# Block transposes on VectorE and sixteen copies in place of TensorE transposes, for three of four batches

## The chip, the cores and the metric

The kernel runs on one core of a Trainium2 chip. The metric is the device time of one execution in microseconds; of the kernel before there are three timed runs and one profiled execution.

## The reference

The inputs are x (4 batches of 512 tokens, 512 wide, float32) and a context of the same shape.

```
xn   = (x - mean) / sqrt(var + eps)                      # layer norm
q, k_new, v_new = xn @ wq.T, xn @ wk.T, xn @ wv.T
k, v = concat(ctx, k_new), concat(ctx, v_new)            # 1024 keys
x    = x + softmax(q @ k.T / sqrt(512)) @ v @ wo.T
xf   = layer_norm(x)
w, idx = top_k(softmax(xf @ gate.T), 6)                  # 64 experts, capacity 128
x    = x + routed experts(xf, w, idx) + shared expert(xf)
```

Every product is done as three passes over numbers split into a high and a low part (high by high, high by low, low by high), each part in a one-pass format. So every operand of TensorE exists twice, as `name_hi` and `name_lo`: ScalarE makes the high part by a copy with rounding, VectorE makes the low part by subtracting the high part from the value.

## The kernel before

**Stages.** Attention and router run batch by batch, then the 64 experts. The function `body` of each engine handles batch b and, while it does, prepares batch b+1: its rows x are loaded, normalised, transposed to `xnT` and projected to q, k and v. Batch 0's own preparation stands ahead of the loop. The last call has `more` false and prepares no batch.

**TensorE's order in a body** (L968 on): transposes of the softmax rows (`pT`), the scores of row tiles 2 and 3, the projections v 1 to 3 of batch b (the last readers of this batch's `xnT`), four groups `av` of 24 matmuls each (attention times values), four groups `wo` of 12 matmuls (the output projection), q 0 and 1 of batch b+1, transposes `x2T` of the second norm, q 2 and 3, the router's logits, k 0 to 3, v 0, the scores of row tile 0, eight short matmuls `pos` that count how many earlier tokens chose each expert, and the scores of row tile 1. In the kernel before, the transposes of the normalised rows stand in this order too: tiles 0 and 1 after `av` 1, tiles 2 and 3 after `av` 3, four 128x128 transposes a tile, by `transposes` at L901 (matmuls against an identity, into a PSUM bank).

**Groups and banks.** Every such product is a group, and the groups take four PSUM banks in turn, by the list `groups_of` (L50). A group's bank is free when the group four places ahead of it has been taken: ScalarE writes the high part (`high`, L447), VectorE subtracts and adds one to `group_taken` (`low`, L578). TensorE waits for that in `claim`; `taken` waits until an operand has been split. The order in which ScalarE and VectorE take groups is written out in their bodies as calls `h(...)` and `l(...)`.

**Weights and context** come through two stage buffers of 1 MB as items, in the order `ctx`, `wo`, `ctxT'`, `wq'`, `wk'`, `wv'`; SyncE loads an item when VectorE has made the low part of the item two places ahead (`load_item`, L287). `high_item` and `low_item` split them, 2048 columns at a time.

**The normalised rows.** `xn` is one tile of 128 partitions by 4 by 512. It is also the router's scratch: `hot` (24 one-hot rows of 64) and `chosen` (the mask) are views of it. At L309 SyncE loads the next rows once all groups of the last body are taken, the two of `pos` among them. VectorE takes statistics (`layernorm_stats`, L585) after v 3, GpSimd raises the variance to the power -1/2 (`first_norm`, L395), and VectorE normalises in place (`layernorm_apply`, L596) after `av` 0.

**The router's mask.** L797 sums the six one-hot rows of each token by four reductions; L800 and L802 make the mask and its running sums, after which TensorE's `pos` group may start (`chosen_ready`). L817 then picks positions with 24 small instructions a batch whose main output goes to `hot` and is not read (only the accumulated column is).

**GpSimd** sends the routed tokens of a batch to the table by 24 indirect DMAs (L421), during the next body. Each waits for a step of TensorE's pace (`paced`: two steps for each scores tile, one for each v group, two for each av group). The norm's power stands in that list ahead of DMA 12.

Of the kernel before, what the change touches and what calls it, by code (L numbers as in the profile page):

```python
# [29 lines left out]
P = 128  # L30
# [11 lines left out]
OVER = float(1 << 20)  # L42

# [6 lines left out]
def groups_of(more):  # L50

    nxt = more * 1
    return (
        [("pT", n) for n in range(6)] + [("v", 1), ("pT", 6), ("pT", 7), ("v", 2), ("v", 3)]
        + [("av", 0), ("av", 1)] + [("xnT", 0), ("xnT", 1)] * nxt + [("av", 2), ("av", 3)]
        + [("xnT", 2), ("xnT", 3)] * nxt + [("wo", i) for i in range(NT)]
        + [("q", 0), ("q", 1)] * nxt + [("x2T", i) for i in range(NT)] + [("q", 2), ("q", 3)] * nxt
        + ([("logitsT", 0), ("k", 0), ("logits", 0), ("k", 1), ("k", 2), ("k", 3), ("v", 0), ("pos", 0), ("pos", 1)]
           if more else [("logits", 0), ("logits", 1), ("pos", 0), ("tab", 0), ("tabw", 0)])
    )  # L60
# [41 lines left out]
def attention_and_router(nc, ctx, sem, t, table, x2_rows, second_sum, x2T_kept, kept):  # L102
# [21 lines left out]
    x2T = tuple(h[:, 0:C, :] for h in pT)  # L124
    pbuf = sb("pbuf", [P, 2, KV])
    x2 = pbuf[:, :, :].rearrange("p a (b d) -> p (a b) d", d=D)
    xn = sb("xn", [P, NT, D])
    logitsT = xn[0:E, 0, :]
# [70 lines left out]
    xn_ready = sem("xn_ready")  # L199
    scores_full = sem("scores_full")  # L200
# [39 lines left out]
    ctx_v = t["ctx"].rearrange("(b i p) d -> b p i d", b=B, p=P)  # L240
    weight_source = {"wq'": t["wqT"], "wk'": t["wkT"], "wv'": t["wvT"], "wo": t["woT"],
# [43 lines left out]

    def sync(sp, before_last_rows):
# [16 lines left out]
        def body(b, more):  # L303
            load_item(b, more, "ctx", b)
            load_item(b, more, "wo")
            if more:

                sp.wait_ge(group_taken, b * PER + len(FIRST) + BANKS)
                sp.dma_start(xn[:, :, :], x_v[b + 1]).then_inc(x_loaded, 16)  # L309
# [3 lines left out]
            if more:  # L313
                for name in ("ctxT'", "wq'", "wk'"):
                    load_item(b, more, name, b + 1)
# [43 lines left out]
    def gpsimd(pool):  # L359
# [40 lines left out]
        def body(b, more):  # L400
# [35 lines left out]
    def scalar(act, two):  # L436
# [21 lines left out]
        def body(b, more):  # L458
# [9 lines left out]
            exp(b, 3)  # L468
            h(("pT", 4), ("pT", 5), ("v", 1), ("pT", 6), ("pT", 7), ("v", 2), ("v", 3))
# [92 lines left out]
    def vector(dve, two):  # L562
# [22 lines left out]
        def layernorm_stats(by_tile=False):  # L585
            for i in range(NT):
                if by_tile:
                    dve.wait_ge(x_tile_loaded[i], 16)
                last = dve.bn_stats(stats[:, i, :], xn[:, i, :])
            link(last)  # L590
            for i in range(NT):
# [101 lines left out]
        def body(b, more):  # L693
# [25 lines left out]
            l(("av", 0))  # L719
            if more:  # L720
                dve.wait_ge(rstd_ready, b * (NT + 1) + 2)
                layernorm_apply()
            l(("av", 1))
# [7 lines left out]
            if more:  # L731
                l(("xnT", 2), ("xnT", 3))
# [63 lines left out]
            for i in range(NT):  # L796
# [14 lines left out]
            for n in range(2):  # L811
# [3 lines left out]
                for i in (2 * n, 2 * n + 1):  # L815
                    for k in range(K):
                        last = dve.scalar_tensor_tensor(  # L817
                            out=hot[:, i * K + k, :], in0=iota_e[:, :], scalar=argf[:, i, k:k + 1],
# [20 lines left out]
        layernorm_stats(by_tile=True)  # L839
# [21 lines left out]
    def tensor(pe, two):  # L861
# [106 lines left out]
        def body(b, more):  # L968
# [5 lines left out]
            def next_xnT(*tiles):  # L974
                for i in tiles:
                    pe.wait_ge(xn_ready, (b + 1) * NT + i + 1)
                    transposes(b, more, ("xnT", i), xn[:, i, :])

# [10 lines left out]
            for m in range(C):  # L989
# [23 lines left out]
            if more:  # L1013
                taken(b, more, ("xnT", NT - 1))
# [787 lines left out]
```

## Time and profile before

| | us |
|---|---|
| median of 3 timed runs | 806.75 (806.72 to 806.81) |
| the profiled execution | 804.55 |
| its span, first to last instruction | 802.8 |
| TensorE busy | 767.4 (96%) |
| VectorE busy | 592.1 (74%) |
| ScalarE busy | 449.4 (56%) |
| GpSimd busy | 319.6 (40%) |

The engines' busy times overlap, so they do not add up to the span. PE is TensorE's matmul side, DVE is VectorE, ACT is ScalarE, POOL is GpSimd, SP is SyncE, which only issues DMAs here; a q behind a name is the engine's instruction queue. Matmuls are pipelined: one of 512 columns is shown as 0.39 us long, while the next starts 0.23 us after it, so time on TensorE is read from the starts. A body lasts 99 us: the first stands at about 50 to 150 us, the second at 150 to 249 and the third at 249 to 348.

### The profile page before, as it was taken

The numbers are of one execution on the slowest core, as the hardware profiler recorded it, in microseconds if no ns is written. First come the engines' busy times: TensorE is split into PE (matmuls) and PEld (weight loads), VectorE is DVE, ScalarE is ACT, GpSimd is POOL, SyncE is SP. The second block draws the span as 40 slices with busy tenths as digits, with TensorE's granted clock in tenths as the row PEclk, the third lists the DMA queues.
The fourth block names the chain that finished last, engine by engine and source line by source line (L and its number), as shares of the span: only waits on it lengthen the run. The fifth ranks groups of instructions, "written<-read, shape, count | busy, mean of one in ns | idle before, by whom it ended". The sixth has DMA issues, their size and how long they took to land.

```text
span 802.8 us, 10922 instructions
## 1 busy us (share of the span) xinstructions
PE 767.4 (96%) x3886; PEld 648.9 (81%) x3886; DVE 592.1 (74%) x1174; ACT 449.4 (56%) x795; POOL 319.6 (40%) x256
## 2 busy tenths in 40 slices
PE   6999999999999999999999999999999999999982
PEld 5888887888878887888888888898988888888762
DVE  6437485875867757676478799999999989999622
ACT  3424323343233333334243799999899888889610
POOL 1000010337103461045423656556565676565440
PEclk9999999999999999999999999999999999999997
DMA  5961236222453225503284999999999999999988
GB/s 167 318 246 54 105 150 217 88 74 103 177 191 106 69 90 200 219 2 109 86 322 158 285 355 343 355 353 344 350 347 351 347 345 349 344 352 349 251 175 195
DMA packets 60292, 181.39 MB, mean 226 GB/s; under 512 B 7680, under 2 KB 8064, under 8 KB 56576
## 3 DMA queue, kind: packets, MB, share of 16 engines
q1 hardware_dynamic: 41184, 139.74, 46.5%
q0 software_dynamic: 19056, 40.98, 22.0%
q8 instruction: 31, 0.51, 0.2%
q14 instruction: 21, 0.17, 0.1%
HBM read 144.38 MB, written 43.92 MB: 235 GB/s over the span
## 4 chain that ended last, share of the span: by engine, by line
PE 59%; DMA 16%; DVE 10%; issue 5%; ACT 4%; POOL 4%; SPq 1%; POOLq 0%; DVEq 0%
PE bank L1097 8%; PE bank L1099 8%; PE bank L1098 8%; DMA raw<-expert_in 7%; DMA stage<-wvT_in 3%; PE scores L1097 3%; PE scores L1099 3%; PE scores L1098 3%; PE ps_gu L1097 3%; PE ps_gu L1099 3%; PE ps_gu L1098 3%; PE bank L904 3%; DMA second_sum<-product,idx_all 3%; DMA second_sum<-eo,idx_all 2%; PE ps_dn L1097 2%
## 5 line engine op out<-in xcount | busy, mean ns | idle before, releaser
L421 POOL DMA_INDIRECT table<-rows,slot x72 | 80.4, 1117 | 157.8 <-DVEq L831 114.1
L1482 DVE TENSOR_TENSOR gu_lo<-raw,gu_hi 128x768 fp32r<-128x768 f32 x126 | 120.3, 956 | 12.9 <-ACT gu_hi L1398 12.1
L1398 ACT ACTIVATE gu_hi<-raw 128x768 fp32r<-128x768 f32 x128 | 107.3, 841 | 10.9 <-DMA raw<-expert_in 10.6
L1097 PE MATMUL ps_gu<-gu_hi,xgT_hi 128*128 128x384 f32 x256 | 91.5, 357 | 0.0
L1099 PE MATMUL ps_gu<-gu_hi,xgT_lo 128*128 128x384 f32 x256 | 86.4, 337 | 0.0
L1098 PE MATMUL ps_gu<-gu_lo,xgT_hi 128*128 128x384 f32 x256 | 86.1, 336 | 0.0
L449 ACT ACTIVATE qT<-bank 128x512 fp32r<-128x512 f32 x32 | 19.2, 600 | 114.7 <-PE bank L1099 109.1
L1342 POOL DMA_INDIRECT xg<-x_rows,idx_all x39 | 47.4, 1216 | 42.3 <-DVEq L667 17.4
L454 ACT ACTIVATE pbuf<-scores,negmax 128x1024 f32<-128x1024 f32 x16 | 17.9, 1118 | 70.2 <-DVE negmax L604 70.2
L582 DVE TENSOR_TENSOR qT<-bank,qT 128x512 fp32r<-128x512 f32 x32 | 22.1, 690 | 47.1 <-ACT qT L449 47.1
L1350 POOL DMA_INDIRECT out_rows<-product,idx_all x25 | 41.3, 1651 | 31.6 <-DMA out_rows<-product,idx_all 14.5
L1098 PEld LDWEIGHTS ps_gu<-gu_lo,xgT_hi 128*128 128x128 f32 x256 | 48.3, 189 | 0.0
L1097 PEld LDWEIGHTS ps_gu<-gu_hi,xgT_hi 128*128 128x128 f32 x256 | 48.2, 188 | 0.0
L1099 PEld LDWEIGHTS ps_gu<-gu_hi,xgT_lo 128*128 128x128 f32 x256 | 48.1, 188 | 0.0
L1482 DVE TENSOR_TENSOR dn_lo<-raw,dn_hi 128x512 fp32r<-128x512 f32 x64 | 44.1, 688 | 2.4 <-ACT dn_hi L1403 1.9
L1482 DVE TENSOR_TENSOR dn_hi<-rest,dn_hi 64x512 fp32r<-64x512 f32 x64 | 44.0, 688 | 0.9
L1097 PE MATMUL bank<-xnT_hi,w_hi 128*128 128x512 f32 x112 | 44.2, 395 | 0.0
L1482 DVE TENSOR_TENSOR xgT_lo<-ps_xgT,xgT_hi 128x512 fp32r<-128x512 f32 x64 | 43.8, 684 | 0.2 <-ACT xgT_hi L1417 0.2
L1099 PE MATMUL bank<-xnT_hi,w_lo 128*128 128x512 f32 x112 | 43.7, 390 | 0.0
L1098 PE MATMUL bank<-xnT_lo,w_hi 128*128 128x512 f32 x112 | 43.6, 389 | 0.0
L398 POOL TENSOR_TENSOR rstd<-veps,half 128x4 f32<-128x4 f32 x4 | 9.9, 2469 | 84.6 <-DVE veps L594 84.6
L582 DVE TENSOR_TENSOR pT_lo<-bank,pT_hi 128x512 fp32r<-128x512 f32 x48 | 30.5, 684 | 16.7 <-ACT pT_hi L449 16.6
(284 smaller groups left out, 2267.5 us busy)
## 6 DMA issues: line engine op xcount, KB each, us to landing
raw<-expert_in SPq DMA_DIRECT2D x64, 1024.0 KB, 13.6
rest<-rest_in SPq DMA_DIRECT2D x32, 256.0 KB, 10.0
x_rows<-pbuf SPq DMA_DIRECT2D x17, 256.0 KB, 2.3
stage<-wkT_in SPq DMA_DIRECT2D x4, 1024.0 KB, 4.9
stage<-ctxT_in SPq DMA_DIRECT2D x4, 1024.0 KB, 4.8
stage<-wvT_in SPq DMA_DIRECT2D x4, 1024.0 KB, 9.0
stage<-ctx_in SPq DMA_DIRECT2D x4, 1024.0 KB, 9.4
stage<-woT_in SPq DMA_DIRECT2D x4, 1024.0 KB, 4.9
```

The lines of the kernel that those rows point to most:

```text
L421: pool.indirect_dma_start(out=table, out_offset=bass.IndirectOffsetOnAxis(ap=slot[:, i, k:k + 1], axis=0), in_=rows[:, i, k, :], in_offset ...
L449: act.activation(split_dest(group)[0], split_source(key, group), ACT.Copy).then_inc(high_done, 1)
L454: act.activation(pbuf[:, i % 2, :], scores[:, i % 2, :], ACT.Exp, bias=negmax[:, i:i + 1], scale=SCALE, accum_out=rowsum[:, i:i + 1]).then ...
L582: dve.tensor_tensor(lo, split_source(key, group), hi.bitcast(F32), ALU.subtract).then_inc(group_taken, 1)
L904: last = pe.transpose(bank_of(key, group)[:, cols(j)], source[:, cols(j)], ident[:, :])
L1097: pe.matmul(out, still[0], moving[0], start=first, stop=False)
L1098: pe.matmul(out, still[0], moving[1], start=False, stop=False)
L1099: return pe.matmul(out, still[1], moving[0], start=False, stop=last)
L1342: pool.indirect_dma_start(out=xg[e % XG], out_offset=None, in_=x2_rows, in_offset=index(("expert", e))).then_inc(gathered[e % XG], 16)
L1350: pool.indirect_dma_start(out=(t["out"], second_sum)[r % 2], out_offset=index(what), in_=eo[r % EO], in_offset=None, compute_op=ALU.add).t ...
L1398: act.activation(gu[n % GU_SLOTS][0][part], gate_up_of(n, part), ACT.Copy).then_inc(weights_high, 1)
L1482: return dve.tensor_tensor(lo, x, hi.bitcast(F32), ALU.subtract)
```

## The change

1. The eight TensorE transposes after `av` 1 and the eight after `av` 3 are gone, with their groups, in the three bodies with `more`.
2. In their place VectorE transposes every 32x32 block of the normalised rows into `blocks`, a view of `pbuf` (the softmax rows, read by then), four instructions of 128x512 after v 3. Sixteen DMAs of 64 KB, each 32 partitions by 4 by 128 numbers, carry the blocks to their partitions, into `xnT_lo`: eight issued by SyncE, eight by ScalarE after it has taken `av` 0. ScalarE then rounds `xnT_lo` into `xnT_hi` and VectorE subtracts in place, four instructions of 128x512 each, after `av` 1 and item `ctxT'`. The rows are loaded in another order of tokens (`x_quads`) so that this comes out right.
3. The load of the next rows, as four DMAs, is issued when the mask of the last batch is made, ahead of item `wo` on SyncE's queue. For this the unread output of L817 goes to a free part of `pT_hi`, and ScalarE waits for the end of that stage (`rows_ready`) before `pT` 4.
4. The statistics are taken earlier: two tiles after the maximum of row tile 2, two after `pT` 3, the variances after the maximum of row tile 3. The rows are normalised after v 2. GpSimd's power stands ahead of DMA 9 instead of DMA 12.
5. The mask is summed by three additions over all tiles (768, 256 and 256 columns) instead of four reductions.

```diff
@@ groups_of
-        + [("av", 0), ("av", 1)] + [("xnT", 0), ("xnT", 1)] * nxt + [("av", 2), ("av", 3)]
-        + [("xnT", 2), ("xnT", 3)] * nxt + [("wo", i) for i in range(NT)]
+        + [("av", m) for m in range(C)] + [("wo", i) for i in range(NT)]
...
+    unused = [pT[0][:, C + m // 4, (m % 4 + 4) * E:(m % 4 + 5) * E] for m in range(2 * K)]
+    blocks = pbuf[:, :, :].rearrange("p a k -> p (a k)").rearrange("p (d t j) -> p d t j", t=NT, j=SQ)
...
+    def tokens_of(a):
+        return tuple(h[:, :, a * P:(a + 1) * P] for h in xnT)
+
+    def move_xnT(queue, b, first, past):
+        queue.wait_ge(group_full, place(b, True, ("v", C - 1)) + 1)
+        queue.wait_ge(xn_blocked, (b + 1) * NT)
+        for a in range(first, past):
+            for q in range(QUADS):
+                here = blocks[a * SQ:(a + 1) * SQ, :, :, :].rearrange("p (c q) t j -> p q c (t j)", q=QUADS)
+                queue.dma_start(plain(tokens_of(a)[1][q * SQ:(q + 1) * SQ, :, :]),
+                                here[:, q, :, :]).then_inc(xnT_moved[a], 16)
@@ SyncE
             load_item(b, more, "ctx", b)
+            if more:
+                if b:
+                    sp.wait_ge(chosen_ready, b)
+                    sp.wait_ge(router_exp, b * 2 * NT)
+                else:
+                    sp.wait_ge(group_taken, place(0, "first", ("xnT", NT - 1)) + 1 + BANKS)
+                for a in range(QUADS):
+                    sp.dma_start(xn[a * SQ:(a + 1) * SQ, :, :], x_quads[b + 1, a]).then_inc(x_loaded, 16)
             load_item(b, more, "wo")
-            if more:
-                sp.wait_ge(group_taken, b * PER + len(FIRST) + BANKS)
-                sp.dma_start(xn[:, :, :], x_v[b + 1]).then_inc(x_loaded, 16)
...
-                for name in ("ctxT'", "wq'", "wk'"):
+                load_item(b, more, "ctxT'", b + 1)
+                move_xnT(sp, b, 0, 2)
+                for name in ("wq'", "wk'"):
@@ GpSimd
-                if i == 2 and b + 2 < B:
-                    first_norm((b + 1) * (NT + 1) + 1)
                 for k in range(K):
+                    if i * K + k == 9 and b + 2 < B:
+                        first_norm((b + 1) * (NT + 1) + 1)
@@ ScalarE
+            act.wait_ge(rows_ready, 2 * b)
             h(("pT", 4), ("pT", 5), ("v", 1), ("pT", 6), ("pT", 7), ("v", 2), ("v", 3))
...
-            h(("av", 0), ("av", 1))
-            if more:
-                h(("xnT", 0), ("xnT", 1))
+            h(("av", 0))
+            if more:
+                move_xnT(act, b, 2, QUADS)
+            h(("av", 1))
+            if more:
                 high_item(b, more, "ctxT'")
+                for a in range(QUADS):
+                    act.wait_ge(xnT_moved[a], (b + 1) * 16 * QUADS)
+                    hi, lo = tokens_of(a)
+                    act.activation(hi, plain(lo), ACT.Copy).then_inc(xnT_high, 1)
             h(("av", 2), ("av", 3))
             if more:
-                h(("xnT", 2), ("xnT", 3))
@@ VectorE
             maximum(b, 2)
+            if more:
+                dve.wait_ge(x_loaded, (b + 1) * 16 * QUADS)
+                tile_stats(0, 2)
             l(("pT", 2), ("pT", 3))
+            if more:
+                tile_stats(2, NT)
             maximum(b, 3)
+            if more:
+                variances()
...
-            l(("v", 2), ("v", 3))
-            if more:
-                dve.wait_ge(x_loaded, (b + 1) * 16)
-                layernorm_stats()
+            l(("v", 2))
+            if more:
+                dve.wait_ge(rstd_ready, b * (NT + 1) + 2)
+                layernorm_apply()
+            l(("v", 3))
+            if more:
+                for i in range(NT):
+                    dve.wait_ge(xn_ready, (b + 1) * NT + i + 1)
+                    dve.transpose(blocks[:, :, i, :], xn[:, i, :].rearrange("p (d j) -> p d j", j=SQ)
+                                  ).then_inc(xn_blocked, 1)
...
-                l(("xnT", 0), ("xnT", 1))
                 low_item(b, more, "ctxT'")
+                for a in range(QUADS):
+                    dve.wait_ge(xnT_high, b * QUADS + a + 1)
+                    hi, lo = tokens_of(a)
+                    dve.tensor_tensor(lo, plain(lo), plain(hi), ALU.subtract).then_inc(xnT_low, 1)
...
-            for i in range(NT):
-                last = dve.tensor_reduce(chosen[:, i, :], hot[:, i * K:(i + 1) * K, :]
-                                         .rearrange("p k e -> p e k"), AX.X, ALU.add)
-            link(last)
+            hot_of = hot.rearrange("p (i k) e -> p i k e", k=K)
+            link(dve.tensor_tensor(hot_of[:, :, 0:3, :], hot_of[:, :, 0:3, :], hot_of[:, :, 3:6, :], ALU.add))
+            link(dve.tensor_tensor(hot_of[:, :, 0, :], hot_of[:, :, 0, :], hot_of[:, :, 1, :], ALU.add))
+            link(dve.tensor_tensor(chosen[:, :, :], hot_of[:, :, 0, :], hot_of[:, :, 2, :], ALU.add))
@@ TensorE
-                if more and m == 1:
-                    next_xnT(0, 1)
-            if more:
-                next_xnT(2, 3)
...
-                taken(b, more, ("xnT", NT - 1))
+                pe.wait_ge(xnT_low, (b + 1) * QUADS)
                 item(b, more, "wq'")
```

## Rows read from the trace of the kernel before

**Rows 1.** The page: engine totals, then granted TensorE clock and DMA share in 40 slices.
```profile
PE 767.4 (96%) x3886; PEld 648.9 (81%) x3886; DVE 592.1 (74%) x1174; ACT 449.4 (56%) x795; POOL 319.6 (40%) x256
PEclk9999999999999999999999999999999999999997
DMA  5961236222453225503284999999999999999988
```
**Rows 2.** TensorE's waits over the span: us in total, times, longest.
```profile
PE bank L904 <- DVE qT L582: 0.6, 3, 0.2
PE bank L1051 <- DVEq L803: 0.6, 3, 0.2
```
**Rows 3.** TensorE in order of time, body 0, av to wo: start, duration in us.
```profile
73.77 0.39 PE L1097 MATMUL bank<-pT_hi,cx 128*128 128x512 f32 x1
...
76.49 0.39 PE L1097 MATMUL bank<-pT_hi,v_hi 128*128 128x512 f32 x1
...
84.42 0.39 PE L1099 MATMUL bank<-pT_hi,v_lo 128*128 128x512 f32 x1
84.65 1.03 PE L904 MATMUL bank<-ident,xn 128*128 128x128 f32 x8
85.44 0.48 PE L1097 MATMUL bank<-pT_hi,cx 128*128 128x512 f32 x1
85.76 0.40 PE L1098 MATMUL bank<-pT_lo,cx 128*128 128x512 f32 x1
...
96.43 1.03 PE L904 MATMUL bank<-ident,xn 128*128 128x128 f32 x8
97.22 0.48 PE L1097 MATMUL bank<-w_hi,qT 128*128 128x512 f32 x1
97.53 0.40 PE L1098 MATMUL bank<-w_lo,qT 128*128 128x512 f32 x1
```
**Rows 4.** TensorE in order of time at the mask, end of body 0.
```profile
143.23 0.39 PE L1098 MATMUL scores<-kT_lo,qT 128*128 128x512 f32 x1
143.45 0.39 PE L1099 MATMUL scores<-kT_hi,qT 128*128 128x512 f32 x1
144.02 0.20 PE L1051 MATMUL bank<-chosen_b,before 128*128 128x64 bf16 x1 [0.18 <-DVEq L803]
```
**Rows 5.** VectorE in order of time at the mask.
```profile
139.59 3.07 DVE L797 TENSOR_REDUCE xn<-xn 128x64 f32<-128x384 f32 x4
142.70 0.29 DVE L800 CAST chosen_b<-xn 128x256 bf16<-128x256 f32 x1
```
**Rows 6.** Additions of 768 and 256 columns elsewhere: ns min/median/max, first and last start.
```profile
L1482 DVE TENSOR_TENSOR gu_lo<-raw,gu_hi x126: 948/955/1019, 439.1 to 752.3; 128x768 fp32r<-128x768 f32 x126
L635 DVE TENSOR_TENSOR product<-xn x3: 418/419/424, 417.8 to 418.4; 128x256 f32<-128x256 f32 x3
```
**Rows 7.** VectorE in order of time, body 0; in brackets idle before and releaser.
```profile
60.52 1.29 DVE L582 TENSOR_TENSOR pT_lo<-bank,pT_hi 128x512 fp32r<-128x512 f32 x2 [1.76 <-ACT pT_hi L449]
63.67 1.23 DVE L603 TENSOR_REDUCE mx<-scores 128x1 f32<-128x1024 f32 x1 [1.87 <-PE scores L1099]
66.85 1.29 DVE L582 TENSOR_TENSOR pT_lo<-bank,pT_hi 128x512 fp32r<-128x512 f32 x2 [1.76 <-ACT pT_hi L449]
74.60 0.69 DVE L582 TENSOR_TENSOR v_lo<-bank,v_hi 128x512 fp32r<-128x512 f32 x1 [1.87 <-ACT v_hi L449]
75.21 2.46 DVE L589 BATCH_NORM_STATS2 stats<-xn 128x6 f32<-128x512 f32 x4
78.19 2.29 DVE L575 TENSOR_TENSOR w_lo<-stage,w_hi 128x2048 fp32r<-128x2048 f32 x1
81.39 1.92 DVE L598 TENSOR_SCALAR xn<-xn,mv,rstd 128x512 f32<-128x512 f32 x4 [0.31 <-POOL rstd L398]
97.26 0.69 DVE L582 TENSOR_TENSOR qT<-bank,qT 128x512 fp32r<-128x512 f32 x1 [4.76 <-ACT qT L449]
```
**Rows 8.** ScalarE in order of time, body 0, taking av 0 to av 2.
```profile
79.41 0.60 ACT L449 ACTIVATE qT<-bank 128x512 fp32r<-128x512 f32 x1 [3.04 <-PE bank L1099]
84.85 0.60 ACT L449 ACTIVATE qT<-bank 128x512 fp32r<-128x512 f32 x1 [4.84 <-PE bank L1099]
91.18 0.60 ACT L449 ACTIVATE qT<-bank 128x512 fp32r<-128x512 f32 x1 [2.95 <-PE bank L1099]
```
**Rows 9.** DMA issues over the span: times, KB each, median us to landing.
```profile
tab<-table SPq DMA_DIRECT2D x1, 64.0 KB, 2.7
stage<-wqT_in SPq DMA_DIRECT2D x3, 1024.0 KB, 4.8
```
**Rows 10.** The line that loads x's first four tiles: issue ns, then landing.
```profile
L336 SPq DMA_DIRECT2D xn<-x_in x4: 388/424/432, 0.9 to 2.3; - x4
DMA to landing us min/median/max: 2.7/3.5/4.4
```
**Rows 11.** GpSimd in order of time, body 1: DMA 8, then the norm's power.
```profile
162.73 0.97 POOL L421 DMA_INDIRECT table<-rows,slot  x1 [1.75 <-PE scores L1099]
...
177.44 2.95 POOL L398 TENSOR_TENSOR rstd<-veps,half 128x4 f32<-128x4 f32 x1 [5.46 <-DVE veps L594]
```

More of the change, by code:

```diff
@@ L42 @@
 OVER = float(1 << 20)
+SQ = 32
+QUADS = P // SQ
 BANKS = 4
@@ L199, in attention_and_router @@
     xn_ready = sem("xn_ready")
+    xn_blocked = sem("xn_blocked")
+    xnT_moved = [sem(f"xnT_moved{a}") for a in range(QUADS)]
+    xnT_high = sem("xnT_high")
+    xnT_low = sem("xnT_low")
     scores_full = sem("scores_full")
@@ L240, in attention_and_router @@
     ctx_v = t["ctx"].rearrange("(b i p) d -> b p i d", b=B, p=P)
+    x_quads = t["x"].rearrange("(b a i j) d -> b a j i d", b=B, a=QUADS, j=SQ)
     weight_source = {"wq'": t["wqT"], "wk'": t["wkT"], "wv'": t["wvT"], "wo": t["woT"],
@@ L583, in low, with tile_stats, first_stats, variances @@
                               ALU.subtract).then_inc(group_taken, 1)
-        def layernorm_stats(by_tile=False):
-            for i in range(NT):
-                if by_tile:
-                    dve.wait_ge(x_tile_loaded[i], 16)
+        def tile_stats(first, past):
+            for i in range(first, past):
                 last = dve.bn_stats(stats[:, i, :], xn[:, i, :])
             link(last)
+        def first_stats():
+            for i in range(NT):
+                dve.wait_ge(x_tile_loaded[i], 16)
+                last = dve.bn_stats(stats[:, i, :], xn[:, i, :])
+            link(last)
+        def variances():
             for i in range(NT):
@@ L707, in body @@
             maximum(b, 2)
+            if more:
+                dve.wait_ge(x_loaded, (b + 1) * 16 * QUADS)
+                tile_stats(0, 2)
             l(("pT", 2), ("pT", 3))
+            if more:
+                tile_stats(2, NT)
             maximum(b, 3)
+            if more:
+                variances()
             l(("pT", 4), ("pT", 5), ("v", 1), ("pT", 6), ("pT", 7))
             low_item(b, more, "ctx")
-            l(("v", 2), ("v", 3))
+            l(("v", 2))
             if more:
-                dve.wait_ge(x_loaded, (b + 1) * 16)
-                layernorm_stats()
+                dve.wait_ge(rstd_ready, b * (NT + 1) + 2)
+                layernorm_apply()
+            l(("v", 3))
+            if more:
+                for i in range(NT):
+                    dve.wait_ge(xn_ready, (b + 1) * NT + i + 1)
+                    dve.transpose(blocks[:, :, i, :], xn[:, i, :].rearrange("p (d j) -> p d j", j=SQ)
+                                  ).then_inc(xn_blocked, 1)
             low_item(b, more, "wo")
@@ L718, in body @@
                 low_item(b, more, "sg")
-            l(("av", 0))
+            l(("av", 0), ("av", 1))
             if more:
-                dve.wait_ge(rstd_ready, b * (NT + 1) + 2)
-                layernorm_apply()
-            l(("av", 1))
-            if more:
-                l(("xnT", 0), ("xnT", 1))
                 low_item(b, more, "ctxT'")
+                for a in range(QUADS):
+                    dve.wait_ge(xnT_high, b * QUADS + a + 1)
+                    hi, lo = tokens_of(a)
+                    dve.tensor_tensor(lo, plain(lo), plain(hi), ALU.subtract).then_inc(xnT_low, 1)
             else:
@@ L731, in body @@
             if more:
-                l(("xnT", 2), ("xnT", 3))
                 low_item(b, more, "wq'")
@@ L795, in body @@
                 l(("k", 2), ("k", 3))
-            for i in range(NT):
-                last = dve.tensor_reduce(chosen[:, i, :], hot[:, i * K:(i + 1) * K, :]
-                                         .rearrange("p k e -> p e k"), AX.X, ALU.add)
-            link(last)
+            hot_of = hot.rearrange("p (i k) e -> p i k e", k=K)
+            link(dve.tensor_tensor(hot_of[:, :, 0:3, :], hot_of[:, :, 0:3, :], hot_of[:, :, 3:6, :], ALU.add))
+            link(dve.tensor_tensor(hot_of[:, :, 0, :], hot_of[:, :, 0, :], hot_of[:, :, 1, :], ALU.add))
+            link(dve.tensor_tensor(chosen[:, :, :], hot_of[:, :, 0, :], hot_of[:, :, 2, :], ALU.add))
             dve.tensor_copy(chosen_b[:, :, :], chosen[:, :, :])
@@ L817, in body @@
                         last = dve.scalar_tensor_tensor(
-                            out=hot[:, i * K + k, :], in0=iota_e[:, :], scalar=argf[:, i, k:k + 1],
+                            out=unused[(i % 2) * K + k], in0=iota_e[:, :], scalar=argf[:, i, k:k + 1],
                             in1=bank_of(more, ("pos", n))[:, (i % 2) * E:(i % 2 + 1) * E],
@@ L838, in vector @@
         dve.nop().then_inc(item_low, 2)
-        layernorm_stats(by_tile=True)
+        first_stats()
+        variances()
         dve.wait_ge(rstd_ready, 1)
@@ L972, in pT_of @@
                     transposes(b, more, ("pT", n), pbuf[:, i % 2, cols(n % 2, 512)])
[L974 to L977, printed above, removed]
             pT_of(0)
```

## The prediction

> **What bounds the kernel now.** I read the page's totals first, then TensorE's waits, then the order of time around each edit. TensorE is busy for 96% of the span, at the full granted clock in all but the last slice [rows 1], and in the attention bodies it hardly waits: the waits that fall in the three bodies the change touches are two kinds of three each, 0.6 us in all per kind [rows 2]. From 73.77 to 84.42 us matmuls start one upon the other, and the same holds up to the next body. So a body is as long as TensorE's list of work, and the reader should see that two things count: what leaves this list, and whether something the list waits for comes later than now. VectorE, ScalarE and the DMAs have slack, and what they gain or lose inside it is worth nothing. The expert stage after the bodies has its DMAs at 9 of 10 and over in most slices [rows 1], but it begins when TensorE and VectorE get there, so a shorter body moves it forward whole.
>
> **Part 1, the transposes that go.** The last matmul of av 1 starts at 84.42, the eight transposes at 84.65, the first of av 2 at 85.44 and its second at 85.76 [rows 3]. Without the transposes the second would start 0.23 after the first, and the first at 84.65. So 85.76 - 84.65 - 0.23 = 0.88 us go. After av 3 it is 97.53 - 96.43 - 0.23 = 0.87. The same eight transposes stand in all three bodies, at two places each: 3 x (0.88 + 0.87) = 5.25 us. This is on the path, since nothing else is waited for there.
>
> **Part 5, the mask.** The eight pos matmuls could start 0.23 after 143.45, that is at 143.68; they start at 144.02 and wait for VectorE's mask [rows 4], which costs 0.34 us. The idle row shows only 0.18 of it, as the matmul before is drawn longer than its place in the pipe. VectorE's four reductions last from 139.59 to 142.70, or 3.1 us with the hand-over [rows 5]. The three additions take 0.96 + 0.42 + 0.42 = 1.8 us by like shapes [rows 6], and with two more hand-overs of some 0.05 us 1.9. The mask comes 1.2 us earlier, more than the 0.34. Bodies 1 and 2 have the same wait: 3 x 0.34 = 1.0 us. If the strided reading made the additions as slow as the reductions, nothing is gained, and that is the lower bound.
>
> **Part 4, statistics in holes.** VectorE idles 1.76 us before pT 2, 1.87 before the maximum of tile 3 and 1.76 before pT 4 [rows 7]. Two tiles of statistics are 2.46/2 = 1.23 us [rows 7], and fit twice; the aggregates, which took from the end of 75.21 + 2.46 to 78.19, are 0.5 us, and fit the third. Normalising (1.92) goes into the hole of 1.87 before v 3, so v_lo is ready at about 75.4 instead of 75.3. TensorE wants it at 76.49, halfway into av 0 [rows 3]. Cost: nothing; if the cover were gone, each piece would cost its own 0.5 to 1.9 us a body. The power on GpSimd is queued behind DMA 8, which ends at 163.7 in body 1 [rows 11]; the variances are there near 165.4 (a body later than 66.4), the power takes 2.95 and ends by 168.4, and normalising wants it after v 2 at 171.7. Indirect DMA 9 and those behind it wait up to 5 us, and nobody waits for them until the next pos.
>
> **Part 3, the earlier load.** In body 0 the four loads go out behind item ctx, in bodies 1 and 2 at about 143.9 behind the mask, each issue taking 0.42 us [rows 10]. Statistics want the rows at 58.8 and 157.8, which leaves 14 us in the later bodies; four such loads landed within 4.4 us at the start [rows 10]. Queued behind them on SyncE are wo, wanted 30 us later, and the residual rows, wanted 50 us later. ScalarE's new wait for rows_ready stands ahead of pT 4 at 165, and the rows are ready by 155. Cost: nothing.
>
> **Part 2, the new path.** It starts when v 3 is split, at 75.4. VectorE's block transposes are not in the trace. From below a pass over 512 columns is 0.48 us (1.92/4, normalising), from above the reduction of 1024 columns, 1.23 [rows 7]. I take 0.69, as for every two-operand pass over 512 columns there: 4 x 0.69 = 2.8, ready at 78.2 (77.3 to 80.3). Item wo's low part then starts when it does now, at 78.19. SyncE issues eight DMAs, 8 x 0.43 = 3.4 us, to 81.6. ScalarE takes av 0 until 80.0 and issues its eight until 83.4, before av 1 is there at 84.85 [rows 8]. A DMA of 64 KB landed in 2.7 us [rows 9], so the last lands at 86.1, and with the next 1 MB load between them (4.8 us, [rows 9]) at 88. Item ctxT' keeps ScalarE until 87.3, then come four roundings at about 0.5 us to 89.5, and VectorE's subtractions end near 92. TensorE wants xnT at q 0, 104.6. That is 12 us of slack.
>
> The nearer deadline is wo 0. It would now start at 96.43 - 0.88 = 95.55, and takes av 2 with its seventh matmul, at 95.55 + 6 x 0.23 = 96.9. ScalarE must finish the roundings before it takes av 2 (0.6), and VectorE the last subtraction before it splits av 2 (0.7 + 0.7). So the last block may land at 95.0 without any loss, and I expect 86 to 88: 7 us of cover. The transposes after av 3 also used to hide the split of av 3. Its low part is done at 97.26 + 0.69 = 97.95 [rows 7], now 0.88 earlier, 97.07, and wo 0 takes it with its tenth matmul, at 95.55 + 9 x 0.23 = 97.6. So 0.5 us is left.
>
> The Trainium skill's page "VectorE: DVE Perf Modes", section "The three transpose paths", gives VectorE 311 ns for a 128x128 bf16 tile in 32x32 blocks. No row here shows it; as an estimate from that page, four such tiles for 512 columns are 1.24 us and the four instructions 5.0, and the sum would stay the same.
>
> **Sum.** 5.25 + 1.0 = 6.3 us off the profiled execution: 804.55 becomes 798.3 and its span 796.5. The runs shown have a median 2.2 us above the profiled execution; the same difference taken, 806.75 - 6.3 = 800.5. From below: 5.25 alone less a loss of 0.3 per body at wo 0, 4.4 off. From above: 6.3 and the 0.2 of the other wait [rows 2] three times, 6.9 off. So 799.9 to 802.4 for this case.
>
> **Rivals.** (a) *The forecast:* all of the new path lies under av and wo. Chance 0.78.
>
> (b) *Half of it is left:* TensorE stands for av 3 at wo 0, or the mask is not earlier. For it: the 0.5 us left there, and that the additions read hot with a stride. Against: both have a margin. 4.4 off at most bad, up to 5.3: 801.5 to 802.4. Chance 0.11.
>
> (c) *The other side: the copies land too late.* ScalarE stands at the wait for xnT_moved, av 2 and av 3 are queued behind it, and wo 0 stands. This costs nothing up to a landing at 95.0, then a microsecond for each, three times; the gain is used up at 95.0 + 6.3/3 = 97.1. If the eight DMAs of ScalarE's queue went one after another, the last would land at 80.0 + 8 x 2.7 = 101.6, and the kernel would take 3 x 6.6 - 6.3 = 13.5 us more: 820.3. Against it: the four loads of x, issued in 1.8 us, landed at most 4.4 us after their issue [rows 10], so DMAs of one queue overlap. For it: no trace here has a copy from SBUF to SBUF between 32 partitions and 32 others, and sixteen small ones share the engines with wq'. Chance 0.06.
>
> A rule speaks for (c). The page "DMA: Bandwidth & Descriptors" of the Trainium skill, section "Rules for kernel authors", wants many small transfers put together into a large one, since those under 64 KB are mostly overhead. These are just 64 KB. The one row of that size agrees that size hardly counts (2.7 us for 64 KB, 4.8 for 1 MB), and whether sixteen overheads add up or overlap is what (c) turns on.
>
> (d) *The expert stage swallows the gain:* if its weight stream set the end by itself, from a point that the bodies don't move, the time would be 806.7. Against it: the DMAs are nearly idle in some slices before it [rows 1], so the stream waits for the bodies' end. Chance 0.05.
>
> **How the numbers follow.** This kernel's measurement can tell about 0.2%, 1.6 us, from no change. (a) and (b) are faster: 0.89. (d) is the same: 0.05. (c) is slower: 0.06. The range is 799.3 to 803.5: (a) and (b) with room for the expert stage to fall a microsecond otherwise. (c) and (d) stay outside, 0.11 together.
>
> **What would show it.** TensorE's list shows no transposes of xn but the router's, av 2's first matmul 0.23 us after av 1's last, and bodies of 99.0 - 2.1 = 96.9 us. The pos row has no idle time before it. VectorE shows four block transposes near 75.4, of 0.5 to 1.2 us. ScalarE's first rounding of xnT starts right behind item ctxT', with no idle time that a DMA ends. I am wrong if TensorE has a wait at wo (L1097) for qT, or at q 0 for xnT_lo, or if the body shortens by less than 1.5 us. I am wrong on part 4 if VectorE waits for x at L589.

## The result and the profile after

| | kernel before | changed kernel |
|---|---|---|
| first comparison, median | 806.74 us (4 runs, 806.45 to 806.81) | 798.70 us (4 runs, 797.51 to 799.64) |
| the profiled execution, and its span | 804.55, 802.8 | 797.51, 795.8 |
| all comparisons of this study | 805.81 (79 runs, 803.04 to 809.38) | 799.0 (16 runs, 795.58 to 800.85) |

The ratio of the first comparison is 0.9902 (0.9887 to 0.9918). The forecast was 800.5 with a range from 799.3: the way is right, the time lies 0.6 us below the range. Over all runs the medians differ by 6.8 us and the means by 7.1; drawing the runs anew at random, with repeats, gives 6.4 to 7.9 for the means. The forecast gain was 6.3.

The page of the changed kernel, first lines as in [rows 1]:

```profile
PE 762.0 (96%) x3838; PEld 645.6 (81%) x3838; DVE 594.0 (75%) x1183; ACT 449.3 (56%) x795; POOL 309.8 (39%) x256
```

TensorE has 48 matmuls fewer and is as busy. Its order of time at the place of [rows 3], after av 1, and at the mask, as [rows 4]:

```profile
82.66 0.39 PE L1143 MATMUL bank<-pT_hi,v_lo 128*128 128x512 f32 x1
82.88 0.39 PE L1141 MATMUL bank<-pT_hi,cx 128*128 128x512 f32 x1
83.11 0.39 PE L1142 MATMUL bank<-pT_lo,cx 128*128 128x512 f32 x1
...
93.53 0.39 PE L1143 MATMUL bank<-pT_hi,v_lo 128*128 128x512 f32 x1
93.76 0.39 PE L1141 MATMUL bank<-w_hi,qT 128*128 128x512 f32 x1
...
139.91 0.39 PE L1143 MATMUL scores<-kT_hi,qT 128*128 128x512 f32 x1
140.14 0.20 PE L1095 MATMUL bank<-chosen_b,before 128*128 128x64 bf16 x1
```

All three joints are 0.23 us wide and none has an idle note: no transposes, no wait at wo, no wait for the mask. VectorE in body 0, to set beside [rows 5] and [rows 7]:

```profile
56.84 1.28 DVE L622 BATCH_NORM_STATS2 stats<-xn 128x6 f32<-128x512 f32 x2
58.75 1.29 DVE L617 TENSOR_TENSOR pT_lo<-bank,pT_hi 128x512 fp32r<-128x512 f32 x2 [0.64 <-ACT pT_hi L478]
...
70.88 1.91 DVE L639 TENSOR_SCALAR xn<-xn,mv,rstd 128x512 f32<-128x512 f32 x4
72.83 0.69 DVE L617 TENSOR_TENSOR v_lo<-bank,v_hi 128x512 fp32r<-128x512 f32 x1
73.44 2.48 DVE L768 STREAM_TRANSPOSE pbuf<-xn 128x512 f32<-128x512 f32 x4
...
136.06 0.95 DVE L849 TENSOR_TENSOR xn<-xn 128x768 f32<-128x768 f32 x1
137.05 0.43 DVE L850 TENSOR_TENSOR xn<-xn 128x256 f32<-128x256 f32 x1
137.51 0.42 DVE L851 TENSOR_TENSOR xn<-xn 128x256 f32<-128x256 f32 x1
137.97 0.29 DVE L852 CAST chosen_b<-xn 128x256 bf16<-128x256 f32 x1
```

The statistics filled their hole (idle before pT 2 fell from 1.76 to 0.64). The mask's sum takes 137.97 - 136.06 = 1.9 us. ScalarE and SyncE around the copies:

```profile
77.70 5.28 ACTq L305 DMA_DIRECT2D xnT_lo<-pbuf  x8
83.08 0.60 ACT L478 ACTIVATE qT<-bank 128x512 fp32r<-128x512 f32 x1 [4.84 <-PE bank L1143]
...
88.29 0.63 ACT L512 ACTIVATE xnT_hi<-xnT_lo 128x512 fp32r<-128x512 f32 x1 [1.25 <-DMA xnT_lo<-pbuf]
```

```profile
76.01 5.30 SPq L305 DMA_DIRECT2D xnT_lo<-pbuf  x8
81.36 0.60 SPq L323 DMA_DIRECT2D stage<-wqT_in  x1
```

Eight issues take 5.3 us. The last copy lands at 88.3, and ScalarE stands 1.25 us for it, which nobody waits for. Each of SyncE's copies landed 2.1 to 2.2 us after its issue; the last of ScalarE's, issued near 83 and behind the 1 MB load of wq' (81.36), took 5. In e5, where wq' goes out behind all copies, the last one lands 2 to 3 us after its issue. This speaks for the load of wq' as what made it late; e5 also changes the queue, so it is not shown by itself.

**Bodies.** The surest measure is a body's length, from the first pT transpose to the next (four of the changed kernel's rows):

```profile
48.97 0.49 PE L957 MATMUL bank<-ident,pbuf 128*128 128x128 f32 x3
...
145.96 0.71 PE L957 MATMUL bank<-ident,pbuf 128*128 128x128 f32 x5
...
243.20 0.49 PE L957 MATMUL bank<-ident,pbuf 128*128 128x128 f32 x3
...
340.17 0.60 PE L957 MATMUL bank<-ident,pbuf 128*128 128x128 f32 x4
```

| kernel | body 0, 1, 2 (us) | median of its runs |
|---|---|---|
| before | 99.00, 99.05, 99.07 | 805.81 |
| changed | 96.99, 97.24, 96.97 | 799.0 |
| changed, second profile (e1) | 96.98, 97.17, 96.97 | |
| changed, third profile (e9) | 97.01, 97.00, 97.00 | |
| transposes put back (e2) | 98.79, 98.79, 99.31 | 805.12 |
| before, start filled (e3) | 98.99, 99.02, 100.21 | 805.65 |
| before, additions alone (e4) | 98.74, 98.70, 98.70 | 804.99 |
| changed, one queue (e5) | 96.96, 97.30, 98.52 | 800.55 |
| changed, 32 copies (e6) | 104.36, 105.75, 106.06 | 823.88 |
| changed, load late (e7) | 97.84, 99.26, 100.94 | 805.46 |
| changed, reductions back (e8) | 97.27, 98.53, 98.13 | 801.03 |
| changed, wvT early (e10) | 97.01, 96.99, 97.00 | 799.13 |
| before, wvT early (e11) | 98.72, 98.70, 98.70 | 804.54 |
| changed, statistics late (e12) | 100.97, 101.82, 99.52 | 810.96 |

Undisturbed, a body is 99.04 - 96.98 = 2.06 us shorter, against 2.1 forecast. What follows the third body takes 802.8 - 347.92 = 454.9 us before and 795.8 - 340.17 = 455.6 after, so the expert stage did not swallow the gain (rival (d)).

The first body of the changed kernel's profile, though, begins 1.8 us earlier (48.97 instead of 50.80). TensorE in three stretches at the start, of before and then of the changed kernel (stretch, length, busy, granted clock, DMA share, GB/s):

```profile
10.00:14.00 4.00, 2.18 (x17) 1.00 0.45 190
14.00:18.00 4.00, 4.00 (x12) 0.57 0.03 9
18.00:22.00 4.00, 4.00 (x19) 1.00 0.53 167
```

```profile
10.00:14.00 4.00, 2.18 (x17) 1.00 0.48 202
14.00:18.00 4.00, 4.00 (x19) 1.00 0.10 28
...
421.50:425.00 3.50, 3.50 (x10) 0.51 1.03 419
```

After the half-idle stretch from 10 to 14 the kernel before went on at the lower level of the clock (1.2 GHz) for 3.4 us, and the changed one did not; it had a low stretch at 421.5 instead, where it lost again, by an estimate of half of 3.5, some 1.7 us. The 14 profiles of this study do not settle whether the change has a part in the start: the low stretch ahead of 19 us stands in all four of the kernel before and its variants (e3, e4, e11), and in five of the ten of the changed kernel and its variants (e1, e2, e5, e8, e12). The changed kernel itself has it in one profile of three. Body 0 begins at 50.0 to 51.4 with it and at 48.6 to 49.1 without. TensorE's work there is the same in both kernels, and with so few profiles a difference like this can be chance.

### The profile page after: what moved, and what is told of

It is laid out like the page before. It is cut to its first block, busy times and chain, and to the rows that moved or that the text cites. A ratio compares the mean times of both kernels' runs of the same rounds, so it can differ in the third digit from the quotient of the medians.

```text
span 795.8 us, 10898 instructions
## 1 busy us (share of the span) xinstructions
PE 762.0 (96%) x3838; PEld 645.6 (81%) x3838; DVE 594.0 (75%) x1183; ACT 449.3 (56%) x795; POOL 309.8 (39%) x256
## 4 chain that ended last, share of the span: by engine, by line
PE 67%; DMA 11%; DVE 8%; ACT 5%; issue 4%; POOL 4%; SPq 0%; POOLq 0%; DVEq 0%
PE bank L1141 10%; PE bank L1142 10%; PE bank L1143 10%; DMA raw<-expert_in 7%; PE scores L1141 3%; PE scores L1143 3%; PE scores L1142 3%; PE ps_gu L1143 3%; PE ps_gu L1141 3%; PE ps_gu L1142 3%; PE bank L957 2%; DVE gu_lo L1526 2%; PE ps_dn L1141 2%; POOL out_rows L1394 2%; POOL second_sum L1394 1%
## 5 line engine op out<-in xcount | busy, mean ns | idle before, releaser
L1445 ACT ACTIVATE dn_hi<-raw 128x512 fp32r<-128x512 f32 x64 | 40.5, 633 | 2.7 <-DVEq L732 2.7
L610 DVE TENSOR_TENSOR w_lo<-stage,w_hi 128x2048 fp32r<-128x2048 f32 x16 | 36.4, 2281 | 7.0 <-ACT w_hi L470 7.0
```

What stands on the lines that cost most here:

```text
L610: dve.tensor_tensor(lo, item_stage(key, name), hi.bitcast(F32), ALU.subtract).then_inc(item_low, 1)
L1445: act.activation(hi[:, 0:D], raw[n % RAW][:, GU:ROW], ACT.Copy)
```

## The experiments

**e1, the changed kernel again.**

> The changed kernel once more. It came out 8.0 us faster at the median where 6.3 were forecast, and one profile shows the three bodies 5.9 us and the last 0.4 us shorter, and TensorE 1.8 us ahead already before the first body, where the profile of before has 3.4 us of low granted clock (from 14.4 us) and this one has none. Theory A (the 1.8 us at the start belong to the clock and come and go from run to run): this profile may have the low stretch at the start again, and the runs then split into some near 800.4 and some near 798.6. Theory B (the start is always without it in the changed kernel): the profile has no low clock between 9 and 20 us, and all runs lie within 797.3 to 799.7 as before.

Measured: 799.29 (6 runs, 795.58 to 800.85), the kernel before beside it 806.02 (29 runs, 803.04 to 809.38), 6.7 apart. The profile has the low clock at the start:

```profile
10.00:14.00 4.00, 2.03 (x16) 1.00 0.36 152
14.00:18.00 4.00, 3.91 (x11) 0.61 0.00 0
```

and body 0 begins at 51.22. Theory B falls. Of theory A the first half holds, the low stretch comes and goes; the runs do not split into two groups, and the profiled one, with the low stretch, is with 798.41 the second fastest. More important is the scatter: the three runs shown before the prediction lay within 0.1 us, while 79 runs of the same kernel cover 6.3 us (standard deviation 1.4).

**e2, eight transposes put back at both places.**

```diff
+                if more and m % 2:
+                    for j in range(8):
+                        pe.transpose(scores[:, 0, cols(j % 4)], ident[:, :], ident[:, :])
```

> The changed kernel with eight 128x128 transposes of the identity put back on TensorE after av 1 and eight after av 3 in the three bodies (into the idle scores bank, read by nobody). This is the price of step 1 alone. My step: 3 x (0.88 + 0.87) = 5.25 us more than the changed kernel, that is 803.9 if the changed one is at 798.7. Rival (the gain comes from the earlier load, the statistics in holes and fewer groups, and TensorE's transposes were nearly free): less than 2.5 us more.

Measured: 805.12, 5.8 more than the changed kernel beside it. The bodies grow by 1.8 each (the third lost 0.5 more to a late wvT, below), where 1.75 was forecast. Step 1 is shown, at its forecast price. With 98.79 a body also lies within 0.1 us of the kernel before with the additions alone (98.70, e4), so the new path through VectorE and the copies costs TensorE next to nothing.

**e3, the kernel before with 16 transposes of the identity in the idle time at the start.**

> The kernel before with 16 more transposes of the identity at the start, after the first four tiles are transposed, where TensorE idles 1.8 us before its first projection. Theory A or B (the low clock at the start costs 1.8 us and follows an idle stretch): the profile shows no low clock between 10 and 20 us, and the time is about 1.8 us under the kernel before, 804.9. Rival C (the start has no part in it, the extra lies in the expert stage): within 0.5 us of the kernel before or later by up to 0.3 us.

Measured: 805.65 against 806.02, which is what rival C expected. But the run does not decide: its profile has a low stretch from 11.5 to 15.0, which begins ahead of the filled place (the 16 transposes run from 13.56 on), behind an earlier wait of 2.0 us. Body 0 begins at 51.40. What share the start has in the gain stays open. Its third body shows something else; TensorE's waits there for the mask, which sum to 1.6 us, are three, the longest 1.3:

```profile
PE bank L1051 <- DVEq L803: 1.6, 3, 1.3
```

**e4, the additions alone in the kernel before.** Edit: part 5 of the change and nothing else.

> The kernel before with part 5 alone: the mask by three additions. My step: 3 x 0.34 = 1.0 us less, 805.7, and no idle time before the pos matmuls. Rival (the mask was not the last thing that pos waited for, or what follows takes it up; the middle body of the changed kernel shortened by 1.8 instead of 2.1): 0.3 us or less.

Measured: 804.99 against 806.02, 1.0 less; bodies of 98.7, no wait before pos. With runs that scatter by 1.4 the median alone proves little; the bodies do: 0.34 us each.

**e5, all sixteen copies on SyncE's queue.**

```diff
-                move_xnT(sp, b, 0, 2)
+                move_xnT(sp, b, 0, QUADS)
...
-            if more:
-                move_xnT(act, b, 2, QUADS)
```

> The changed kernel with all sixteen copies issued by SyncE, none by ScalarE. In the changed kernel an issue of such a copy takes 0.6 us, the first eight go out from 76.0 us on, and TensorE's wo 0 begins at 93.5, so the last copy may land at 93.0 without loss. Theory (the copies overlap and lie under av): the sixteenth is issued by 76.0 + 16 x 0.66 = 86.6 and lands near 89, and the time is that of the changed kernel (799.3 in the last comparison) within 0.7. Rival (c) of the prediction (copies of one queue follow one another, 2.1 us or more each): the last lands at 76 + 16 x 2.1 = 109.6 and each body loses some 16 us, 845 in all.

Measured: 800.55 (6 runs, 797.64 to 802.96), 1.3 more than the changed kernel's 799.3 and so outside the 0.7 of my theory, but six runs that scatter by 2.2 cannot tell the two kernels apart; two bodies of three are as in the changed kernel. SyncE's order of time, with the copies of body 0, then ScalarE's rounding of the last block:

```profile
77.70 10.37 SPq L305 DMA_DIRECT2D xnT_lo<-pbuf  x16
...
89.56 0.63 ACT L510 ACTIVATE xnT_hi<-xnT_lo 128x512 fp32r<-128x512 f32 x1 [0.83 <-DMA xnT_lo<-pbuf]
```

The copies of one queue overlap: one goes out each 0.65 us and the sixteenth has landed at 89.5, not at 109.6. Rival (c) in its strong form is out.

The third body is 1.5 us longer than the changed kernel's. VectorE stands there ahead of the maximum of tile 2, and the profile names nothing on this core that ended it:

```profile
253.65 1.22 DVE L642 TENSOR_REDUCE mx<-scores 128x1 f32<-128x1024 f32 x1 [2.10 <-remote]
```

The same stands in the third body of e6 (2.44 us), e8 (1.00) and e12 (1.64), and in none of the four profiles of the kernel before and its variants nor in the three of the changed kernel. Its cause is open, and so is whether the change makes it more frequent.

**e6, the same with 32 copies of 32 KB.**

```diff
+                for c in (0, 2):
+                    queue.dma_start(plain(tokens_of(a)[1][q * SQ:(q + 1) * SQ, c:c + 2, :]),
+                                    here[:, q, c:c + 2, :]).then_inc(xnT_moved[a], 16)
```

> As the one before, with each copy cut into two of 32 KB: 32 copies from SyncE, the same bytes. Theory 1 (an issue costs 0.6 us whatever it carries): the last is issued at 76.0 + 32 x 0.62 = 95.8 and lands at 98, 5 us after the last moment without loss, and with three bodies the kernel takes about 15 us more than the changed one, 814; TensorE then shows a wait for qT at its first wo matmul. Theory 2 (an issue costs by the runs that it describes, 128 of them in 64 KB): 0.3 us each, the last lands near 89 and the time is that of the changed kernel.

Measured: 823.88 (5 runs), 24.6 more than the changed kernel. SyncE's order of time in body 0:

```profile
75.63 20.53 SPq L306 DMA_DIRECT2D xnT_lo<-pbuf  x32
```

SyncE's order of time above: an issue costs 0.64 us with half the bytes too (theory 1). The place is the forecast one, TensorE at wo for av (its waits: sum, count, longest):

```profile
PE bank L1140 <- DVE qT L616: 14.7, 3, 5.6
```

and around it (columns as above):

```profile
88.00:98.00 10.00, 6.90 (x31) 1.00 0.24 54
98.00:104.80 6.80, 5.33 (x13) 0.50 0.71 299
104.80:112.00 7.20, 7.20 (x33) 1.00 0.19 73
```

The waits are 14.7 us, as I expected. Of the other 10 most are the clock. It fell inside each of the three waits (here at 98.0, while TensorE waited from 94.9 to 99.5) and stayed at the lower level for 6.8 us, of which TensorE worked 5.3, 5.8 and 5.1. Half of that, 8.1 us, is lost, by an estimate from these lengths. Two more waits of 1.8 us in the third body, behind VectorE's stand there, make 14.7 + 8.1 + 1.8 = 24.6.

**e7, the load of the rows back at its old place.**

```diff
             load_item(b, more, "wo")
+            if more:
+                sp.wait_ge(group_taken, b * PER + len(FIRST) + BANKS)
+                for a in range(QUADS): ...
```

> The changed kernel with the load of the next rows back behind item wo and behind the last group of the body (as four DMAs), all else as changed. Before, this load went out at 153.9 in body 1, and the statistics now want it at 153.9 too (VectorE's maximum of tile 2 ends there in the changed kernel, near 153.8, the load near 150). Theory (VectorE's wait lies under ScalarE's softmax and TensorE's queue): rows land at about 156, VectorE stands 2 us, pT 2 is split 1 to 2 us later, and TensorE, which wants its bank at pT 6, loses nothing: within 0.5 us of the changed kernel. Rival (the early load is needed): VectorE's stand of 2 us moves the maximum of tile 3 and with it TensorE: 2 us in each of two bodies, 4 us more.

Measured: 805.46 (12 runs), 6.2 more. My theory was wrong and the rival right about the place; the loss is larger than its 4 us. VectorE, body 1:

```profile
157.97 1.29 DVE L617 BATCH_NORM_STATS2 stats<-xn 128x6 f32<-128x512 f32 x2 [3.06 <-DMA xn<-x_in]
159.29 1.29 DVE L612 TENSOR_TENSOR pT_lo<-bank,pT_hi 128x512 fp32r<-128x512 f32 x2
```

The rows landed at 158, 6.9 us after the first issue at 151.1; the residual rows are loaded beside them (issued at 152.9), which may be the reason and is not shown. pT 2 and the maximum of tile 3 stand behind that wait, then ScalarE's softmax, then TensorE (1.1 us for the softmax rows, 0.6 for pT_lo in this body). VectorE waits for the rows in all three bodies (2.0, 3.1 and 2.4 us). The third body loses the most, 4.0 us, and part of that is again the clock, low from 266.2 to 269.7 (some 1.7 us by an estimate, half of that stretch):

```profile
266.00:270.00 4.00, 4.00 (x11) 0.57 0.03 5
```

So statistics in VectorE's holes are only free with the early load.

**e8, the reductions back in the changed kernel.** Edit: part 5 undone.

> The changed kernel with the mask by four reductions again. Theory (parts add up): 3 x 0.34 = 1.0 us more than the changed kernel, 0.34 us before each pos matmul. Rival (the wait before pos follows the landing of wvT, which varies from run to run; one profile showed a wait of 1.3): 1.5 us or more on the median, and a wider spread of the runs than the changed kernel has.

Measured: 801.03 (7 runs, 798.73 to 804.78), 1.7 more than the changed kernel had in e1. The rival asked for 1.5 or more and a wider spread, and has both, but runs that scatter by 2.4 do not decide between 1.0 and 1.7. Two bodies of this one profile tell where it comes from. ScalarE's wait for wvT, then TensorE's for the mask, body 0 and body 1:

```profile
125.84 1.92 ACT L470 ACTIVATE w_hi<-stage 128x2048 fp32r<-128x2048 f32 x1 [5.27 <-DMA stage<-wvT_in]
...
224.38 1.92 ACT L470 ACTIVATE w_hi<-stage 128x2048 fp32r<-128x2048 f32 x1 [6.54 <-DMA stage<-wvT_in]
```

```profile
142.41 0.20 PE L1095 MATMUL bank<-chosen_b,before 128*128 128x64 bf16 x1 [0.18 <-DVEq L855]
...
240.94 0.20 PE L1095 MATMUL bank<-chosen_b,before 128*128 128x64 bf16 x1 [1.26 <-DVEq L855]
```

Where wvT lands 1.2 us later, the wait is 1.1 longer. The changed kernel has such a body too (body 1, ScalarE idle 6.46) and pays 97.24 - 96.98 = 0.26 for it (0.5 in e2), where the reductions pay 98.53 - 97.27 = 1.26. The third body's 98.13 has no late wvT; there VectorE stood 1.0 us as in e5. Among the 30 bodies of the ten profiles that load wvT at its old place with no wait at wo, ScalarE's idle time is 5.2 to 6.1 us in 24 and 6.3 to 6.6 in six.

**e9, the changed kernel a third time.**

> The changed kernel a third time, for its median. By the traces so far the three bodies give 3 x 2.07 us, and the mask something more in a body where wvT lands 1.2 us later (then a kernel with the four reductions waits 1.3 us before pos, and one with the additions loses 0.25): one body in four or five of those profiled, so 6.2 + 0.5 = 6.7 us in the mean. Theory D (this is the whole effect, and the 8.0 us of the first comparison are chance of a few runs that scatter by 2 us each way): 6 to 7.5 us under the kernel before. Rival (the change has a further gain outside the bodies, such as at the start): 7.7 us or more again.

Measured: 799.10 (6 runs, 795.97 to 800.44), against 805.30 (17 runs): 6.2, and 6.7 in the means. No body is lengthened in the profile, and it has none of the low clock at the start. The median is theory D's.

**e10 and e11, wvT loaded early**, in the changed kernel and in the kernel before.

```diff
-                for name in ("wq'", "wk'"):
+                for name in ("wq'", "wk'", "wv'"):
                     load_item(b, more, name, b + 1)
...
-                load_item(b, more, "wv'")
```

> The changed kernel with item wvT loaded right behind wkT, ahead of the stores of the rows, instead of behind the stores of x2T; it lands well before it is wanted. Theory D: no body with a late landing, each 96.97 us, 0.1 to 0.3 us less than the changed kernel in the mean, which can't be told from it; ScalarE no longer idles 5.3 us for it. Rival (ScalarE's 5 us for wvT also hold the splits of k and q that TensorE's 0.2 us waits follow, or the load collides with the stores that TensorE's list needs): 1 us less, or 0.5 us more.

> The kernel before with item wvT loaded early in the same way and nothing else changed. If the wait before pos is the end of a chain from wvT's landing through ScalarE's and VectorE's splits to the mask: no wait before pos, bodies of 98.70, and 1.0 to 1.5 us less than the kernel before, as with the additions alone. Rival (the chain runs from the logits, and wvT only stands beside it): the wait of 0.34 us stays in every body, but never 1.3.

Measured: e10 799.13 (6 runs, 797.44 to 799.80), equal to the changed kernel. e11 804.54 (12 runs) against 805.30, bodies of 98.70 and no wait before pos: the same bodies as with the additions. So the wait for the mask was the end of a chain from wvT's landing, and either cure takes it away. A version better than the changed kernel did not come out of it.

**e12, part 4 undone:** statistics, power, normalising and block transposes at the old, later places.

> The changed kernel with part 4 undone: statistics of the next rows after v 3, the power ahead of indirect DMA 12, normalising and block transposes behind item wo's low part; load, copies and mask as changed. The blocks are then ready about 84.4 in body 0 instead of 75.9, ScalarE stands for them before its eight issues until then and issues to 89.7, the last copy lands at 92 to 95, and the last moment without loss is 93.0. Theory (the landing decides, as in the kernel with 32 copies): wo 0 or its av operands come 1 to 3 us late in each body and a stretch of low clock may follow, 3 to 15 us more than the changed kernel, 802 to 814. Rival (part 4 is not needed, the cover of 7 us that the prediction counted takes it up): within 0.7 us of the changed kernel.

Measured: 810.96 (6 runs, 810.02 to 816.03) against 806.02: 12 us more than the changed kernel and slower than the kernel before. ScalarE's order of time in body 0:

```profile
84.94 5.58 ACTq L305 DMA_DIRECT2D xnT_lo<-pbuf  x8
90.56 0.60 ACT L478 ACTIVATE qT<-bank 128x512 fp32r<-128x512 f32 x1 [11.41 <-issue]
91.05 1.91 ACT L470 ACTIVATE ctxT_hi<-stage 128x2048 fp32r<-128x2048 f32 x1
92.86 2.18 ACT L512 ACTIVATE xnT_hi<-xnT_lo 128x512 fp32r<-128x512 f32 x4
94.94 1.07 ACT L478 ACTIVATE qT<-bank 128x512 fp32r<-128x512 f32 x2
```

ScalarE stood for the blocks and then issued, until 90.5; ctxT' and four roundings came behind, and av 2 at 94.94. The copies had landed by then; the late thing is ScalarE's queue. TensorE waited 7.5 us in all at wo (2.2, 3.0 and 2.3), and the clock fell for 3.4 us behind two of the three waits.

## Why the prediction was wrong, point by point

- **What bounds it:** right. Bodies shortened by what left TensorE's list. One reading was too coarse: the digit 9 in [rows 1] covers 90% and over, and a stretch of 3.4 us at the lower clock, from 14.4 us on, lay in the first slices.
- **Part 1, 5.25 us:** right. 98.71 (additions alone) - 96.98 = 1.73 a body, 5.2 in all; 5.8 by the medians of e2, with a scatter of the runs that does not tell the two apart.
- **Part 5, 1.0 us:** the mechanism was right, the size is the smaller of the two failed steps. I read the wait of 0.34 us in three bodies of one execution and took it as fixed. It is the end of a chain from a DMA's landing that in one body of five comes 1.2 us later; there the additions save 1.3. By an estimate from these bodies the mean is 3 x 0.34 + 3 x 0.2 x 1.0 = 1.6. With 5.2 that is 6.8, inside the measured 6.4 to 7.9. The medians alone gave 1.0 (e4), 1.7 (e8) and 0.8 (e11) and cannot tell 1.0 from 1.6.
- **Parts 3 and 4, "cost: nothing":** right in the profiles of the changed kernel, and they earned what I did not credit them with: without the early load 6.2 us are lost, with late statistics 12. The "7 us of cover" of part 2 were their work.
- **Part 2:** the block transposes took 0.62 us each (0.69 taken). An issue took 0.65 us, not 0.43: I had read its price from loads out of HBM. Whether the kind of copy sets it, or what is on the queue already, is not shown: the load of wq' right behind the eight copies took 0.60 too, and 0.34 in the kernel before. The last copy landed at 88.3, with the body shifted by 1.8 that is 90.1 on the old scale, against 86 to 88; the limit of 95 was kept. The 0.5 us left at wo held: no wait. The estimate of 1.24 us for one from the Trainium skill's page "VectorE: DVE Perf Modes", section "The three transpose paths", is twice what this trace has.
- **Rival (b)** did not come: no wait at wo and none before pos. **Rival (c)** did not come either. Its first half, copies one after another, is refuted by e5; its second half, what a late landing costs and where, is confirmed by e6. There the last block landed at 97.4 with body 0 beginning 2.2 us earlier, which is 4.6 past my limit of 95.0, and TensorE waited 4.6. What I left out is that the clock adds to the wait. That e6's 823.9 lies near the 820.3 of rival (c) is luck, as the copies came late for another reason. The Trainium skill's page "DMA: Bandwidth & Descriptors", section "Rules for kernel authors", wants small transfers put together. The runs agree in direction: the price here is 0.64 us for each issue (e5, e6), hidden while there are sixteen of them.
- **The range, "799.9 to 802.4" and 799.3 as its end:** the larger failed step. Its base was the median of three runs within 0.1 us, 806.75; over 79 runs it is 805.8. That is 0.9 of the 1.4 us between the forecast, 806.75 - 6.3, and the changed kernel's 799.0; the gain, 6.8 instead of 6.3, is the other 0.5. The first comparison's 798.7 lies 0.3 further down, by the chance of four runs. And the bounds knew only terms of the sum and "a microsecond" for the expert stage, no scatter of 1.4 us a run, though the profiled execution itself, 2.2 us under the three runs, was a sign of it.
- **The first comparison's 8.0 us** is four runs on either side of kernels that scatter by 1.4 and 1.5. Whether something more than the bodies' 6.8 belongs to the change, such as a share of the start, stays open; the runs do not resolve it.

## What to carry to other kernels

Where one engine's list sets the length, work taken off it is worth its width in the list, and the new path is free only as long as each of its stages lies in a hole; here the holes were made by moving two other things earlier. A wait shown by one execution is one draw: ask what ends the chain behind it, and if that is a DMA, price the wait for a late landing too. Three runs that agree within 0.1 us do not bound the scatter of later ones.

## What the runs showed of the hardware

- An issue of a copy between 32 partitions and 32 others took 0.60 to 0.70 us on SyncE and ScalarE, with 64 KB (e5) or 32 KB (e6) in it. Loads of 256 KB to 1 MB mostly took 0.33 to 0.45, but the one right behind the copies took 0.60 as well.
- In the three waits of 4.5 to 5.6 us of TensorE inside busy work (e6) the clock fell before the wait ended and stayed at the lower level for 6.8 us each time; waits of 2.2 to 3.0 us (e12) were followed by 3.4 us at the lower level in two cases of three.
- The changed kernel's start had 3.4 us at the lower level in one profile of three and none in the others.
